# Attention pass on one Trainium2 core: three bf16 passes for the output projection, the value bias moved into the projection's bias row, and value transfers issued ahead of key transfers

## The chip, the core and the metric

The kernel runs on one core of one Trainium2 chip. The metric is the device time of one execution in microseconds (us). The core has a tensor engine (PE; its weight loads are shown apart, as PEld), a vector engine (DVE), a scalar engine (ACT), a general engine (POOL) and a synchronising engine (SP), which here only issues DMA transfers. Each engine works through its own instructions strictly in the order in which they were written. Engines meet only through semaphores: an instruction waits until a counter has reached a value, and everything that is queued behind it on its engine waits too.

## What is computed

Two layers over x of 128 sequences, 64 tokens and 256 channels. The change touches only the attention of the first layer:

```
x1 = LN(x) * (scale1 + 1) + shift1                  # scale1, shift1, gamma1 come from cond
q, k, v = x1 @ Wqkv + (q_bias, 0, v_bias)           # 16 heads of 16 channels
q = l2norm(q) * exp(min(scale_mul, log 100));  k = l2norm(k)
probs = softmax(q @ k^T)                            # per sequence and head, 64 x 64
o = probs @ v
x = x + (o @ Wproj + proj_b) * gamma1
```

Rows of probs sum to one, so a bias on v adds the same vector v_bias to every row of o, and (o + v_bias) @ Wproj + proj_b equals o @ Wproj + (proj_b + v_bias @ Wproj). A feed-forward part and a second layer of linear attention follow; the change leaves them as they are.

## The kernel before

The program is a setup and three passes in a row, each with a block of its own: attention, feed-forward, linear attention. A block begins only when all engines have finished the one ahead.

**A tile** is two sequences, 128 rows on the 128 partitions; there are 64 tiles. Most products are formed from operands split into a bf16 high part and a bf16 remainder: an engine writes the high part (HI), another subtracts it from the full value and writes the remainder (LO), and PE adds three products, HI*HI + HI*LO + LO*HI (`SPLITS`). The output projection is the exception: its operands are fp32.

**The order of work** in the attention pass is written out by hand. `pipeline(engine, stages)` takes a list of (lag, stage). In step S of the loop the engine runs each stage in the order of the list, on tile S - lag. Steps 0 to 75 are run; a middle part is a hardware loop of four steps a round. So within a step the list is the engine's queue order, and a wait holds all stages behind it. The lists before are:

- PE: scores (lag 8), project (11), turn_qk (5), probs_v (9), turn_o (10), qkv (3), turn_x (1)
- DVE: biases (4), modulate (2), v_low (4), outputs (10), reduce_norms (4), residual (11), hat (1), qk_lo (5), statistics (-1), aggregate (0)
- ACT: v_hi (4), square (4), modulate_second (2), high_exponentials (8), qk_hi (5), x1_high (2), full_exponentials (8), logs (4), o_copy (10), factor (4)
- POOL: normalise (5), rstd_of (1), add (12), x1_low (2), e_lo (8)
- SP: load_gain (9), place_k (5), place_v (5), each for two tiles in every second step

**Where the stages meet.** `qkv` (L779, L784, L787) writes a tile's products; the value half needs a matmul with the bias row (L784) ahead of its six. `v_hi` (ACT, L661) and `v_low` (DVE, L835) split it. `place_v` (L571) moves the split value of two tiles to `v_pairs` in 4 transfers, `place_k` (L553) the key to `k_pairs` in 8. A tile's slot of the split value is overwritten four tiles later, so `v_hi` waits until the transfers of that pair have landed. In the steady loop `place_v` itself waits only for `pv_done`, and `place_k` for `qk_lo_made`. `scores` (L760) waits for the key transfers; `high_exponentials` (L695) and `full_exponentials` (L700) write the exponential in bf16 and in fp32; `e_lo` (POOL, L627) subtracts one from the other, 1024 elements a partition. `probs_v` (L745), `outputs` (DVE, L840 and L845), `turn_o` (L734, a transpose into the second half of the bank `ps_x`) and `o_copy` (ACT, L706, to fp32) follow. `project` (PE, L722 and L724) needs `o_copy`, and the value split of the same step: its result shares a bank with the value, so it waits for `v_lo_made` of tile S - 4. `turn_qk` (L770), `qk_hi` (L681), `qk_lo` (L873) turn and split query and key. `residual` (DVE, L829) multiplies the projected tile by gamma1, `hat` (DVE, L881) normalises the next tile of x, SBUF to SBUF in fp32. The value half of `qkv` waits for `residual` of the same step, since they share the bank.

Of the kernel before, what the change touches and what calls it, by code (L numbers as in the profile page):

```python
# [22 lines left out]
ALU = mybir.AluOpType  # L23
# [83 lines left out]
class Shared:  # L107


    def __init__(self, nc, ctx):  # L110
        def sb(name, shape, dt):
# [14 lines left out]
        self.w_proj = sb("w_proj", [P, NC_, C], F32)  # L126
# [19 lines left out]
        self.bias_rows = sb("bias_rows", [P, 5 * C], BF16)  # L146
        self.rows_v, self.rows_proj, self.rows_qv3, self.rows_out3 = (
            self.bias_rows[:, a * C:b * C] for a, b in ((0, 1), (1, 2), (2, 4), (4, 5)))
# [13 lines left out]
def setup(nc, m, x, cond, qkv_w, q_bias, v_bias, scale_mul, proj_w, proj_b, ada_w, ada_b,  # L162
# [3 lines left out]
    with ExitStack() as ctx:  # L166
# [23 lines left out]
        bias_full = sb("bias_full", [P, 5 * C])  # L190
        bias_rest = sb("bias_rest", [P, 5 * C])
        bias_high = sb("bias_high", [P, 5 * C], BF16)
        bias_mid = sb("bias_mid", [P, 5 * C], BF16)
        band = sb("band", [P, P])
        ps = [ctx.enter_context(nc.psum_tensor(f"set_ps{i}", [P, 512], F32)) for i in range(6)]
# [9 lines left out]
        qkv_here = sem("qkv_here")  # L205
        qkv_hi_made = sem("qkv_hi_made")
# [25 lines left out]
        def _(sp):  # L232
            load(sp, [(cond_sb[:], cond)], cond_here)
            load(sp, [(w_ada[:], ada_w.rearrange(CHUNKED, p=P))], ada_here)
# [3 lines left out]
            load(sp, [(m.w_proj[:], proj_w.rearrange(CHUNKED, p=P))], attention_here)  # L238
# [5 lines left out]
            sp.wait_ge(attention_here, 16 * 2)  # L244

        @block.scalar
        def _(act):
            load(act, [(head_scale[:], scale_mul.rearrange("a h b c -> (a b c) h").to_broadcast([P, H]))], heads_here)
            load(act, [(bias_full[:, i * C:(i + 1) * C], row(b)) for i, b in enumerate((v_bias, proj_b, bq, bv, out_b))],
# [16 lines left out]
            act.activation(m.w_qkv[:, HI], qkv_full[:], ACT.Copy).then_inc(qkv_hi_made, 1)  # L266

        @block.gpsimd
        def _(pool):
# [24 lines left out]
            pool.tensor_tensor(m.w_qkv[:, LO], qkv_full[:], m.w_qkv[:, HI], ALU.subtract)  # L294
            pool.wait_ge(biases_split, 1)
# [7 lines left out]
        def _(pe):  # L303
# [5 lines left out]
            last.then_inc(transposed, 1)  # L309
            pe.wait_ge(cond_t_made, 1)  # L310
# [20 lines left out]
        def _(dve):  # L331
            dve.wait_ge(heads_here, 16)
# [13 lines left out]
            dve.wait_ge(biases_here, 16 * 5)  # L346
# [56 lines left out]
def attention_pass(nc, m, x, fc1_w):  # L403
# [10 lines left out]
    with ExitStack() as ctx:  # L414
# [30 lines left out]
        o_t = sb("o_t", [P, 2, SEQ, L])  # L445
# [13 lines left out]
        ps_xt, ps_ot = ps_x[:, 0:C], ps_x[:, C:2 * C]  # L459
        ps_vv, ps_y = ps_v[:, 0:C], ps_v[:, C:2 * C]  # L460
# [39 lines left out]
        o_t_made = sem("o_t_made")  # L500
# [18 lines left out]
        def _(sp):  # L519
# [56 lines left out]
            pipeline(sp, [(9, load_gain), (5, place_k), (5, place_v), (0, load_later)])  # L576
# [57 lines left out]
        def _(act):  # L634
# [67 lines left out]
            def o_copy(t):  # L702
                a = t.slot(2)
                act.wait_ge(o_turned, t.n + 1)
                reuse(act, proj_done, t, 2)
                act.activation(o_t[a][:], ps_ot.rearrange("p (s g q) -> p g s q", s=SEQ, g=2), ACT.Copy  # L706
                               ).then_inc(o_t_made, 1)
# [4 lines left out]
                           (2, x1_high), (8, full_exponentials), (4, logs), (10, o_copy), (5, split_fc1),  # L712
# [3 lines left out]
        def _(pe):  # L716
            def project(t):
                a = t.slot(2)
                pe.wait_ge(o_t_made, t.n + 1)
# [53 lines left out]
            def qkv(t):  # L773
# [976 lines left out]
```

## Time and profile before

| What | Value |
|---|---|
| Median of 3 runs | 1348.47 us (1347.26 to 1349.31) |
| Profiled execution: its own time, its span | 1349.81 us, 1347.9 us |
| Granted TensorE clock, mean share of full speed | 0.967 |
| PE busy | 1152.5 us, 86% |
| PEld busy | 856.6 us, 64% |
| DVE busy | 994.8 us, 74% |
| ACT busy | 867.3 us, 64% |
| POOL busy | 933.9 us, 69% |
| Setup | 0 to about 38.8 us |
| Attention pass | about 38.8 to 527 us |
| The two other passes | about 527 to 1347.9 us |

The busy shares are means over passes with different limits; the change lies in the first two stretches only. A timeline row gives the start in us, the time in us, engine, line, operation, what is written and read, the shapes and the count; a bracket behind it tells how long the engine stood idle ahead of it and which operation let it go. Consecutive operations of one engine overlap a little, so the distance from one start to the next is often shorter than the duration.

### The profile page before, as it was taken

How to read it: one execution, taken by the hardware profiler on the slowest of the kernel's cores; microseconds unless marked ns; L12 is line 12 of the kernel's file. 1: busy time of each engine (PE TensorE's matmuls, PEld its weight loads, DVE VectorE, ACT ScalarE, POOL GpSimd, SP SyncE). 2: the span in 40 equal slices, each digit the busy share in tenths (PEclk: the TensorE clock that was granted, in tenths of full speed). 3: DMA queues.
4: the chain of work that ended last, by engine and by line, in shares of the span. 5: the costliest groups of instructions: out<-in, count | busy, mean ns of one | idle time of the engine just before them, and what ended most of it. 6: DMA issues, size and time to landing. Idle time of an engine off the chain costs nothing. (4 is left out here: it accounts for less than half of the span.)

```text
span 1347.9 us, 38178 instructions
## 1 busy us (share of the span) xinstructions
PE 1152.5 (86%) x12189; PEld 856.6 (64%) x12342; DVE 994.8 (74%) x2388; ACT 867.3 (64%) x2268; POOL 933.9 (69%) x1091
## 2 busy tenths in 40 slices
PE   2568898998989874899999999978888888888886
PEld 1356777777777763466666666655666666666664
DVE  2857787887878754745556465439999999999993
ACT  1456677777777762545454544528888888888884
POOL 3547677777777755656575765635788888888888
PEclk9789999999999997899999999989999999999997
DMA  5454233232333332110101001000011111111112
GB/s 149 152 112 117 56 52 62 54 60 56 57 61 53 65 54 66 40 32 16 32 16 31 18 29 32 17 16 7 24 37 51 35 35 50 36 37 36 52 36 71
DMA packets 142704, 67.73 MB, mean 50 GB/s; under 512 B 80688, under 2 KB 141360, under 8 KB 142640
## 3 DMA queue, kind: packets, MB, share of 16 engines
q1 hardware_dynamic: 109472, 40.53, 14.2%
q10 hardware_dynamic: 33168, 26.38, 6.9%
q8 instruction: 35, 0.57, 0.2%
q14 instruction: 29, 0.24, 0.1%
HBM read 41.18 MB, written 8.65 MB: 37 GB/s over the span
## 5 line engine op out<-in xcount | busy, mean ns | idle before, releaser
L1107 PE MATMUL f_ps_y<-w_fc,f_h_split 128*128 128x256 bf16 x1536 | 172.7, 273 | 1.4 <-DVE f_branch L1213 1.4
L1134 PE MATMUL f_ps_h<-f_x_split,w_fc 128*128 128x512 bf16 x737 | 165.8, 381 | 3.1 <-DVE f_x_split L1187 1.5
L1107 PEld LDWEIGHTS f_ps_y<-w_fc,f_h_split 128*128 128x128 bf16 x1536 | 150.2, 98 | 22.5 <-issue 1.7
L627 POOL TENSOR_TENSOR e_split<-e_full,e_split 128x1024 bf16<-128x1024 f32 x64 | 136.6, 2135 | 32.7 <-ACT e_full L700 31.6
L1221 DVE TENSOR_TENSOR f_h_split<-f_h,f_h_split 128x512 bf16<-128x512 f32 x64 | 65.0, 1018 | 103.0 <-ACT f_h L1091 103.0
L1090 ACT ACTIVATE f_h_split<-f_ps_h,b_fc 128x512 bf16<-128x512 f32 x128 | 89.0, 695 | 66.0 <-POOL f_h_split L1045 32.6
L1134 PEld LDWEIGHTS f_ps_h<-f_x_split,w_fc 128*128 128x128 bf16 x768 | 75.4, 98 | 87.0 <-issue 2.2
L609 POOL TENSOR_TENSOR x_split<-x_t,x_split 128x256 bf16<-128x256 f32 x64 | 44.6, 697 | 104.4 <-ACT x_split L649 104.4
L760 PE MATMUL ps_s<-qk_t,k_pairs 128*128 128x64 bf16 x3072 | 101.7, 194 | 11.7 <-DMA k_pairs<-qk_t 9.8
L760 PEld LDWEIGHTS ps_s<-qk_t,k_pairs 128*128 128x128 bf16 x3072 | 99.0, 99 | 14.5 <-DMA k_pairs<-qk_t 11.0
L1045 POOL TENSOR_TENSOR f_h_split<-f_h,f_h_split 128x512 bf16<-128x512 f32 x64 | 80.6, 1269 | 36.3 <-ACT f_h L1091 36.3
L1560 PE MATMUL l_ps_qv<-w_qvk,l_x_split 128*128 128x512 bf16 x383 | 94.4, 383 | 4.9 <-DVE l_v_split L1672 1.5
L661 ACT ACTIVATE v_split<-ps_v 128x256 bf16<-128x256 f32 x64 | 24.8, 387 | 108.1 <-DMA v_pairs<-v_split 86.6
L1091 ACT ACTIVATE f_h<-f_ps_h,b_fc 128x512 f32<-128x512 f32 x128 | 89.5, 699 | 0.0
L779 PE MATMUL ps_qk<-w_qkv,x_split 128*128 128x512 bf16 x323 | 83.3, 390 | 5.3 <-POOL x_split L609 1.1
L1078 ACT ACTIVATE f_x_split<-f_x 128x1024 bf16<-128x1024 f32 x16 | 16.9, 1057 | 107.9 <-POOL f_x L1000 107.9
L1430 ACT ACTIVATE l_z_t<-l_ps_yt,shift,scale 128x64 f32<-128x64 f32 x256 | 83.5, 425 | 4.3 <-PE l_ps_yt L1509 3.2
L1464 ACT ACTIVATE l_kq<-l_ps_k,l_k_shift 128x64 f32<-128x64 f32 x256 | 76.9, 313 | 11.5 <-DVE l_k_shift L1652 11.5
L695 ACT ACTIVATE e_split<-ps_s,minus_shift 128x1024 bf16<-128x1024 f32 x64 | 71.5, 1117 | 10.2 <-PE ps_s L760 9.9
L1521 PE MATMUL l_ps_y<-l_kv_split,l_kq_t 128*64 128x128 bf16 x768 | 41.6, 222 | 39.8 <-DVE l_y_hat L1609 39.8
L1368 POOL TENSOR_TENSOR l_kv_split<-l_kv,l_kv_split 128x512 bf16<-128x512 f32 x64 | 73.9, 1155 | 0.2 <-ACT l_kv_split L1443 0.2
L1450 ACT ACTIVATE l_kq_t<-l_ps_kq 128x512 bf16<-128x512 f32 x64 | 38.2, 597 | 53.1 <-PE l_ps_kq L1549 53.1
(171 smaller groups left out, 3416.1 us busy)
## 6 DMA issues: line engine op xcount, KB each, us to landing
v_pairs<-v_split SPq DMA_DIRECT2D x128, 66.0 KB, 2.1
k_pairs<-qk_t SPq DMA_DIRECT2D x256, 32.0 KB, 2.2
gain<-gammas SPq DMA_DIRECT2D x64, 128.0 KB, 3.0
f_gain<-gammas ACTq DMA_DIRECT2D x32, 256.0 KB, 4.3
l_gate<-in_cond ACTq DMA_DIRECT2D x128, 64.0 KB, 2.6
out<-x_all ACTq DMA_DIRECT2D x16, 512.0 KB, 2.9
x_all<-in_x SPq DMA_DIRECT2D x13, 512.0 KB, 6.5
w_ada<-in_L_cond_ada_w SPq DMA_DIRECT2D x1, 1536.0 KB, 8.3
```

Source lines behind the costliest of these rows:

```text
L627: pool.tensor_tensor(flat(e_split[a][:, LO]), flat(e_full[:]), flat(e_split[a][:, HI]), ALU.subtract).then_inc(e_lo_made, 1)
L760: last = pe.matmul(ps_s[:, s, G_ * c + g], k_pairs[:, t.slot(4), k, c, s, g].rearrange("p r k -> p (r k)"), qk_t[:, 0, t.slot(4), q, c, s ...
L779: last = pe.matmul(ps_qk[:, :], x1_split[a][:, xs, c, :], m.w_qkv[:, ws, c, 0:2 * C], start=(i == 0 and c == 0), stop=(i == 2 and c == NC_ ...
L1045: pool.tensor_tensor(h_split[a][:, LO, f], h[f % 4][:], h_split[a][:, HI, f], ALU.subtract).then_inc(h_lo_odd, 1)
L1090: act.activation(h_split[a][:, HI, f], ps_h[f % 4][:], ACT.Gelu, bias=m.b_fc1[:, f:f + 1])
L1091: act.activation(h[f % 4][:], ps_h[f % 4][:], ACT.Gelu, bias=m.b_fc1[:, f:f + 1]).then_inc(h_made, 1)
L1107: last = pe.matmul(ps_y[:, i], h_split[a][:, hs, f, i * P:(i + 1) * P], m.w_fc2[:, ws, f], start=(f == 0 and k == 0), stop=(f == F_CHUNKS ...
L1134: last = pe.matmul(ps_h[f % 4][:], m.w_fc1[:, ws, c, f * P:(f + 1) * P], x2_split[a][:, xs, c], start=(k == 0 and c == 0), stop=(k == 2 an ...
L1368: pool.tensor_tensor(kv_split[a][:, LO], kv[a][:], kv_split[a][:, HI], ALU.subtract).then_inc(kv_lo_made, 1)
L1430: act.activation(z_t[a][:, c, s * L:(s + 1) * L], ps_yt[:, c, s * L:(s + 1) * L], ACT.Identity, bias=by_seq(m.shift3, c, t, s), scale=by_s ...
L1464: act.activation(kq[t.slot(4)][:, i * L:(i + 1) * L], ps_k[:, c, s * L:(s + 1) * L], ACT.Exp, bias=k_shift[a][:, c, s:s + 1], accum_out=su ...
L1560: last = pe.matmul(ps_qv[:], x3_split[a][:, xs, c], m.w_qvk3[:, ws, c, 0:2 * C], start=False, stop=(i == 2 and c == NC_ - 1))
```

## The change

1. **Projection.** The projection weight is split in the setup into bf16 high part and remainder. `o_copy` becomes `o_hi` (ACT, same place in its list, writes bf16), and a new stage `o_low` on DVE subtracts it from the transposed output in PSUM. `project` runs six bf16 matmuls of 256 columns in place of two fp32 ones (four entries in the trace). What waited for `o_t_made` (`project`, `turn_o`, `turn_x`) waits for `o_lo_made`.
2. **Value bias.** The setup forms v_bias @ Wproj with two fp32 matmuls on a widened bias and adds it to proj_b; the row of v_bias goes from the loop, and with it one matmul of 256 columns a tile. The bias buffers hold 4 rows of 256 instead of 5.
3. **Transfers.** `place_v` stands ahead of `place_k` in SP's list.

The diff, without declarations:

```diff
@@ -231,22 +239,23 @@
             load(sp, [(cond_sb[:], cond)], cond_here)
+            load(sp, [(proj_full[:], proj_w.rearrange(CHUNKED, p=P))], proj_here)
             load(sp, [(w_ada[:], ada_w.rearrange(CHUNKED, p=P))], ada_here)
...
             load(sp, [(w_emb[:], emb_w.rearrange(CHUNKED, p=P))], emb_here)
-            load(sp, [(m.w_proj[:], proj_w.rearrange(CHUNKED, p=P))], attention_here)
             sp.wait_ge(gammas_made, 1)
...
             load(sp, [(m.x_all[:, part], x_tiles(x)[:, part])], m.x_here[1])
-            sp.wait_ge(attention_here, 16 * 2)
+            sp.wait_ge(attention_here, 16)

...
             load(act, [(head_scale[:], scale_mul.rearrange("a h b c -> (a b c) h").to_broadcast([P, H]))], heads_here)
-            load(act, [(bias_full[:, i * C:(i + 1) * C], row(b)) for i, b in enumerate((v_bias, proj_b, bq, bv, out_b))],
+            load(act, [(b_v[:], column(v_bias))], proj_here)
+            load(act, [(bias_full[:, i * C:(i + 1) * C], row(b)) for i, b in enumerate((proj_b, bq, bv, out_b))],
                  biases_here)
@@ -264,6 +273,8 @@
             act.activation(m.w_qkv[:, HI], qkv_full[:], ACT.Copy).then_inc(qkv_hi_made, 1)
+            act.wait_ge(proj_here, 16 * 2)
+            act.activation(m.w_proj[:, HI], proj_full[:], ACT.Copy).then_inc(proj_hi_made, 1)

@@ -292,6 +303,8 @@
             pool.tensor_tensor(m.w_qkv[:, LO], qkv_full[:], m.w_qkv[:, HI], ALU.subtract)
+            pool.wait_ge(proj_hi_made, 1)
+            pool.tensor_tensor(m.w_proj[:, LO], proj_full[:], m.w_proj[:, HI], ALU.subtract)
             pool.wait_ge(biases_split, 1)
@@ -307,6 +320,11 @@
             last.then_inc(transposed, 1)
+            pe.wait_ge(v_bias_widened, 1)
+            pe.wait_ge(proj_here, 16 * 2)
+            for c in range(NC_):
+                last = pe.matmul(ps[5][:, 0:C], b_v_wide[:, c], proj_full[:, c], start=(c == 0), stop=(c == NC_ - 1))
+            last.then_inc(v_bias_carried, 1)
             pe.wait_ge(cond_t_made, 1)
@@ -329,6 +347,8 @@
         def _(dve):
+            dve.wait_ge(proj_here, 16 * 2)
+            dve.tensor_copy(b_v_wide[:], b_v[:, :, None].to_broadcast([P, NC_, P])).then_inc(v_bias_widened, 1)
             dve.wait_ge(heads_here, 16)
@@ -343,7 +363,10 @@

-            dve.wait_ge(biases_here, 16 * 5)
+            dve.wait_ge(biases_here, 16 * 4)
+            dve.wait_ge(v_bias_carried, 1)
+            dve.tensor_tensor(bias_full[:, 0:C], bias_full[:, 0:C], ps[5][:, 0:C], ALU.add).then_inc(proj_bias_summed, 1)
+            dve.wait_ge(proj_bias_summed, 1)
             dve.tensor_copy(bias_high[:], bias_full[:]).then_inc(biases_split, 1)
@@ -457,6 +480,7 @@
         ps_xt, ps_ot = ps_x[:, 0:C], ps_x[:, C:2 * C]
+        turned_o = ps_ot.rearrange("p (s g q) -> p g s q", s=SEQ, g=2)
         ps_vv, ps_y = ps_v[:, 0:C], ps_v[:, C:2 * C]
@@ -573,7 +598,7 @@

-            pipeline(sp, [(9, load_gain), (5, place_k), (5, place_v), (0, load_later)])
+            pipeline(sp, [(9, load_gain), (5, place_v), (5, place_k), (0, load_later)])
             sp.wait_ge(x_updated, TILES)
@@ -699,36 +724,36 @@

-            def o_copy(t):
+            def o_hi(t):
                 a = t.slot(2)
...
                 reuse(act, proj_done, t, 2)
-                act.activation(o_t[a][:], ps_ot.rearrange("p (s g q) -> p g s q", s=SEQ, g=2), ACT.Copy
-                               ).then_inc(o_t_made, 1)
+                act.activation(o_t[a][:, HI], turned_o, ACT.Copy).then_inc(o_hi_made, 1)

...
             pipeline(act, [(4, v_hi), (4, square), (2, modulate_second), (8, high_exponentials), (5, qk_hi),
-                           (2, x1_high), (8, full_exponentials), (4, logs), (10, o_copy), (5, split_fc1),
+                           (2, x1_high), (8, full_exponentials), (4, logs), (10, o_hi), (5, split_fc1),
                            (4, factor)])
...
                 a = t.slot(2)
-                pe.wait_ge(o_t_made, t.n + 1)
+                pe.wait_ge(o_lo_made, t.n + 1)
                 reuse(pe, branch_made, t, 1)
...
                 pe.matmul(ps_y, m.ones[:], m.rows_proj, start=True, stop=False)
-                for g in range(2):
-                    last = pe.matmul(ps_y, o_t[a][:, g].rearrange("p s q -> p (s q)"), m.w_proj[:, g, :],
-                                     start=False, stop=(g == 1))
+                for i, (os, ws) in enumerate(SPLITS):
+                    for g in range(2):
+                        last = pe.matmul(ps_y, o_t[a][:, os, g].rearrange("p s q -> p (s q)"), m.w_proj[:, ws, g],
+                                         start=False, stop=(i == 2 and g == 1))
                 last.then_inc(proj_done, 1)
...
                 pe.wait_ge(o_made, t.n + 1)
-                reuse(pe, o_t_made, t, 1)
+                reuse(pe, o_lo_made, t, 1)
                 bank_free(pe, x1_second, t, 8, SEQ)
@@ -781,18 +806,17 @@
                 bank_free(pe, branch_made, t, -8)
-                pe.matmul(ps_vv, m.ones[:], m.rows_v, start=True, stop=False)
                 for i, (xs, ws) in enumerate(SPLITS):
...
                         last = pe.matmul(ps_vv, x1_split[a][:, xs, c, :], m.w_qkv[:, ws, c, 2 * C:3 * C],
-                                         start=False, stop=(i == 2 and c == NC_ - 1))
+                                         start=(i == 0 and c == 0), stop=(i == 2 and c == NC_ - 1))
                 last.then_inc(qkv_done, 1)
...
                 reuse(pe, x1_second, t, 1, SEQ)
-                bank_free(pe, o_t_made, t, -9)
+                bank_free(pe, o_lo_made, t, -9)
                 for c in range(NC_):
@@ -847,6 +871,12 @@

+            def o_low(t):
+                a = t.slot(2)
+                dve.wait_ge(o_hi_made, t.n + 1)
+                reuse(dve, proj_done, t, 2)
+                dve.tensor_tensor(o_t[a][:, LO], turned_o, o_t[a][:, HI], ALU.subtract).then_inc(o_lo_made, 1)
+
             def statistics(t):
@@ -893,7 +923,7 @@
             pipeline(dve, [(4, biases), (2, modulate), (4, v_low), (10, outputs), (4, reduce_norms),
-                           (11, residual), (1, hat), (5, qk_lo), (-1, statistics), (0, aggregate), (1, clear_k)])
+                           (10, o_low), (11, residual), (1, hat), (5, qk_lo), (-1, statistics), (0, aggregate), (1, clear_k)])

```

DVE, a step of the attention pass in the fill of the pipeline, from the norms of query and key to the next value split (L808/L832 and L810/L834 norms, L829/L853 `residual`, L881/L911 `hat`, L873/L903 `qk_lo`), before:

```order
L808 TENSOR_REDUCE norms<-squares 128x32 [waits logs_made,squared]
L810 SCALAR_TENSOR_TENSOR norms<-norms,norm_weight 128x32 [waits norms_made]
L829 TENSOR_TENSOR branch<-ps_v,gain 128x256 [waits gain_here0,proj_done]
L881 TENSOR_SCALAR x_hat<-x_all,mean_var,rstd 128x256 [waits x_hat_t,rstd_made]
L873 TENSOR_TENSOR qk_t<-ps_qkt,qk_t 128x2x256 [waits qk_hi_made]
```

and after:

```order
L832 TENSOR_REDUCE norms<-squares 128x32 [waits logs_made,squared]
L834 SCALAR_TENSOR_TENSOR norms<-norms,norm_weight 128x32 [waits norms_made]
L878 TENSOR_TENSOR o_t<-ps_x,o_t 128x256 [waits o_hi_made]
L853 TENSOR_TENSOR branch<-ps_v,gain 128x256 [waits gain_here0,proj_done]
L911 TENSOR_SCALAR x_hat<-x_all,mean_var,rstd 128x256 [waits x_hat_t,rstd_made]
L903 TENSOR_TENSOR qk_t<-ps_qkt,qk_t 128x2x256 [waits qk_hi_made]
```

The new row L878 (`o_low`) with its wait for ACT stands ahead of `residual`, `hat` and `qk_lo`.

SP, one round of the steady loop (two of its four steps), before:

```order
L529 DMA gain<-gammas 64x2x256
L548 ISA
L553 DMA k_pairs<-qk_t 16x16x64 [waits qk_lo_made]
L553 DMA k_pairs<-qk_t 16x16x64 x7
L571 DMA v_pairs<-v_split 64x2x264 [waits pv_done]
L571 DMA v_pairs<-v_split 64x2x264 x3
```

and after:

```order
L554 DMA gain<-gammas 64x2x256
L413 ISA
L596 DMA v_pairs<-v_split 64x2x264 [waits pv_done]
L596 DMA v_pairs<-v_split 64x2x264 x3
L573 REGISTER_ALU
L578 DMA k_pairs<-qk_t 16x16x64 [waits qk_lo_made]
L578 DMA k_pairs<-qk_t 16x16x64 x7
```

The four value transfers and their wait stand ahead of the eight key transfers.

## Rows read from the trace of the kernel before

**Rows 1.** List of waits, 100 to 450 us: total us, times, longest us.

```profile
ACT v_split L661 <- DMA v_pairs<-v_split: 66.6, 25, 4.8
```

**Rows 2.** Timeline, end of a step; columns: start us, us, engine, line, operation.

```profile
299.59 1.11 ACT L700 ACTIVATE e_full<-ps_s,minus_shift 128x1024 f32<-128x1024 f32 x1
299.72 2.61 SPq L571 DMA_DIRECT2D v_pairs<-v_split  x4
299.77 0.67 POOL L609 TENSOR_TENSOR x_split<-x_t,x_split 128x256 bf16<-128x256 f32 x1 [0.36 <-ACT x_split L649]
...
299.83 0.76 DVE L881 TENSOR_SCALAR x_hat<-x_all,mean_var,rstd 128x256 f32 x1
300.51 0.68 DVE L873 TENSOR_TENSOR qk_t<-ps_qkt,qk_t 128x512 bf16<-128x512 f32 x1
...
300.70 0.38 ACT L706 ACTIVATE o_t<-ps_x 128x256 f32<-128x256 f32 x1
300.77 2.14 POOL L627 TENSOR_TENSOR e_split<-e_full,e_split 128x1024 bf16<-128x1024 f32 x1 [0.33 <-ACT e_full L700]
...
300.99 0.82 PE L787 MATMUL ps_v<-w_qkv,x_split 128*128 128x256 bf16 x6
301.11 0.41 DVE L860 BATCH_NORM_STATS2 stats<-x_all 128x6 f32 x1
...
301.52 0.65 DVE L888 TENSOR_TENSOR qk<-ps_qk,b_qk 128x512 f32<-128x512 f32 x1
...
301.64 0.38 PE L797 MATMUL ps_x<-ident,x_hat 128*128 128x128 f32 x2
```

**Rows 3.** Timeline, the step after it and part of the next.

```profile
303.82 0.39 ACT L661 ACTIVATE v_split<-ps_v 128x256 bf16<-128x256 f32 x1 [2.52 <-DMA v_pairs<-v_split]
...
304.36 0.43 DVE L835 TENSOR_TENSOR v_split<-ps_v,v_split 128x256 bf16<-128x256 f32 x1 [1.46 <-ACT v_split L661]
...
304.84 0.28 PE L722 MATMUL ps_v<-bias_rows,ones 128*128 128x256 bf16 x1 [1.42 <-DVE v_split L835]
...
304.96 1.03 PE L724 MATMUL ps_v<-w_proj,o_t 128*128 128x256 f32 x4
...
305.83 0.60 PE L770 MATMUL ps_qkt<-ident,qk_hat 128*128 128x128 f32 x4
...
306.46 0.60 ACT L681 ACTIVATE qk_t<-ps_qkt 128x512 bf16<-128x512 f32 x1
...
306.90 0.42 DVE L829 TENSOR_TENSOR branch<-ps_v,gain 128x256 f32<-128x256 f32 x1
...
307.24 0.40 DVE L881 TENSOR_SCALAR x_hat<-x_all,mean_var,rstd 128x256 f32 x1
307.26 1.11 ACT L700 ACTIVATE e_full<-ps_s,minus_shift 128x1024 f32<-128x1024 f32 x1
...
308.27 5.28 SPq L553 DMA_DIRECT2D k_pairs<-qk_t  x8
...
309.54 1.56 PE L760 MATMUL ps_s<-qk_t,k_pairs 128*128 128x64 bf16 x48
...
309.88 0.60 DVE L820 TENSOR_SCALAR x_t<-ps_x,scale,shift 128x64 f32<-128x64 f32 x2 [0.43 <-PE ps_x L797]
310.39 0.42 DVE L835 TENSOR_TENSOR v_split<-ps_v,v_split 128x256 bf16<-128x256 f32 x1
...
312.35 0.91 PE L745 MATMUL ps_o<-v_pairs,e_split 128*128 128x66 bf16 x24
```

**Rows 4.** Instructions of line 829 (the branch), whole program; durations ns min/median/max.

```profile
L829 DVE TENSOR_TENSOR branch<-ps_v,gain x64: 423/424/426, 99.7 to 525.7; 128x256 f32<-128x256 f32 x64
```

**Rows 5.** Timeline, the branch of the last step that still splits a value.

```profile
492.97 0.42 DVE L829 TENSOR_TENSOR branch<-ps_v,gain 128x256 f32<-128x256 f32 x1
```

**Rows 6.** Busy times of one window: us busy (count) per engine, PE clock, DMA.

```profile
110.00:120.00 10.00, 7.30 (x135) 6.05 (x132) 6.28 (x16) 4.79 (x11) 8.20 (x11) 1.00 0.50 84
```

**Rows 7.** Timeline of the setup: the widest step of the bias split.

```profile
25.97 4.32 DVE L349 TENSOR_TENSOR bias_rest<-bias_full,bias_high 128x1280 f32<-128x1280 f32 x1
```

More of the change, by code:

```diff
@@ L125, in __init__ @@
         self.w_qkv = sb("w_qkv", [P, 2, NC_, 3 * C], BF16)
-        self.w_proj = sb("w_proj", [P, NC_, C], F32)
+        self.w_proj = sb("w_proj", [P, 2, NC_, C], BF16)
         self.w_fc1 = sb("w_fc1", [P, 2, NC_, D_FF], BF16)
@@ L145, in __init__ @@
         self.ones = sb("ones", [P, P], BF16)
-        self.bias_rows = sb("bias_rows", [P, 5 * C], BF16)
-        self.rows_v, self.rows_proj, self.rows_qv3, self.rows_out3 = (
-            self.bias_rows[:, a * C:b * C] for a, b in ((0, 1), (1, 2), (2, 4), (4, 5)))
+        self.bias_rows = sb("bias_rows", [P, 4 * C], BF16)
+        self.rows_proj, self.rows_qv3, self.rows_out3 = (
+            self.bias_rows[:, a * C:b * C] for a, b in ((0, 1), (1, 3), (3, 4)))
         self.b_fc1 = sb("b_fc1", [P, D_FF // P], F32)
@@ L189, in setup @@
         qkv_full = sb("qkv_full", [P, NC_, 3 * C])
[L190 to L193, printed above, removed]
+        bias_full = sb("bias_full", [P, 4 * C])
+        bias_rest = sb("bias_rest", [P, 4 * C])
+        bias_high = sb("bias_high", [P, 4 * C], BF16)
+        bias_mid = sb("bias_mid", [P, 4 * C], BF16)
         band = sb("band", [P, P])
+        proj_full = sb("proj_full", [P, NC_, C])
+        b_v = sb("b_v", [P, NC_])
+        b_v_wide = sb("b_v_wide", [P, NC_, P])
         ps = [ctx.enter_context(nc.psum_tensor(f"set_ps{i}", [P, 512], F32)) for i in range(6)]
@@ L205, in setup @@
         qkv_here = sem("qkv_here")
+        proj_here = sem("proj_here")
+        proj_hi_made = sem("proj_hi_made")
+        v_bias_widened = sem("v_bias_widened")
+        v_bias_carried = sem("v_bias_carried")
+        proj_bias_summed = sem("proj_bias_summed")
         qkv_hi_made = sem("qkv_hi_made")
@@ L444, in attention_pass @@
         o_full = sb("o_full", [P, SEQ, C // 2], F32, 1)[0]
-        o_t = sb("o_t", [P, 2, SEQ, L])
+        o_t = sb("o_t", [P, 2, 2, SEQ, L], BF16)
         gain = sb("gain", [P, 4, C], F32, 1)[0]
@@ L499, in attention_pass @@
         o_turned = sem("o_turned")
-        o_t_made = sem("o_t_made")
+        o_hi_made = sem("o_hi_made")
+        o_lo_made = sem("o_lo_made")
         proj_done = sem("proj_done")
@@ L1729, in laid_out @@
         return a.reshape(1, 2, H // 2, 1).swapaxes(1, 2).reshape(1, H, 1, 1)
+    if name == "L0_cond_v_bias":
+        return a.reshape(2, H // 4, 2, HD).transpose(2, 1, 0, 3).reshape(C)
     if name == "L0_cond_proj_w":
```

## The prediction

> **What bounds the kernel now.** I read the busy table first: PE leads with 86%, but as a mean over three passes. The change touches the setup and the attention pass, so I read the list of waits of the steady part of that pass. Its largest wait that holds up everybody is one for a transfer: ACT's `v_hi` waits 66.6 us, in 25 waits, for value transfers to land, once in two steps [rows 1]. The timeline shows how [rows 2, 3]. In the step that begins with the scores near 302 us, the four value issues end at 299.72 + 2.61 = 302.33, ACT gets on at 303.82, that is 1.49 later, and DVE's `v_low` (304.36) and PE's projection (304.84) follow in a row. The next step has no such wait: from one `v_low` to the next, 304.36 to 310.39, it is 6.03 us. The mean step is longer: the branch of step 11 starts at 99.7 and that of step 67 at 492.97 [rows 4, 5], 393.3 us for 56 steps, 7.02 a step. The sum has to say what the 56 become.
>
> **The projection on PE.** From the bias matmul to the transposes behind it are 305.83 - 304.84 = 0.99 us [rows 3]. The new form keeps the bias matmul (0.12 to the next start) and has six bf16 matmuls of 256 columns, the form of the value half, 301.64 - 300.99 = 0.65 [rows 2]. That is 0.77, so 0.22 less. The value half loses its bias matmul, another 0.12. PE gets 0.34 a step, worth something only where PE ends last.
>
> **The new stage on DVE.** `o_low` has exactly the form of `v_low` (PSUM and bf16 in, bf16 out, 256 elements), 0.43 us [rows 3]; 0.34 to the next start, as from the branch to `hat`, 306.90 to 307.24. The cost is not in the 0.34 but in its place. It waits for `o_hi` of the same step, and ACT reaches that copy only behind `full_exponentials`: 299.59 to 300.70, 1.11 after that one's start [rows 2]. In the step of rows 3 DVE has done its branch at 306.90 and its `hat` at 307.24, before ACT has even begun `full_exponentials` (307.26). Queued behind the new wait are `residual`, `hat`, `qk_lo`, `statistics`, and then `biases`, `modulate` and `v_low` of the next step. The projection of the next step waits for that `v_low`, `turn_qk` is behind the projection, `qk_hi` behind `turn_qk`, and `full_exponentials` and `o_hi` behind `qk_hi`. So the wait closes a ring through all of DVE's second half, PE and ACT, once a step, without slack.
>
> **A hold within the ring.** `hat` now comes while POOL runs `e_lo`, which it never does in the rows of before. When they meet, it costs. At 299.83 `hat` was recorded with 0.76 us instead of 0.40, while POOL's fp32-to-bf16 subtraction ran from 299.77 to 300.44 [rows 2, 3]: its own 0.40 began at 300.19, 0.25 ahead of POOL's recorded end. `e_lo` is the same kind of subtraction, four times as long. The statistics at 301.11 ran at 0.41 in the middle of an `e_lo`, so not every DVE operation is held; those that read PSUM are not either (301.52, 0.65) [rows 2].
>
> The Trainium skill, SBUF — State Buffer, section "SBUF: two separate sides", says that VectorE and GpSimd share a pair of ports by an exclusive lock, held for the whole instruction of the one that came first. The trace agrees that `hat` is held, but has it start 0.25 before the recorded end; by the page's rule to the letter each step would be 0.25 longer and the sum 1427.
>
> **The ring, added up** from the start of `full_exponentials` to the next. `e_lo` starts 300.77 - 299.59 = 1.18 later and takes 2.14; `hat` gets on 0.25 before its end: 3.07. Then `qk_lo` 0.32 (300.51 - 300.19), `statistics` 0.60 (301.11), `biases` 0.41 (301.52), all [rows 2]; `modulate` 0.60, as for the other 512-element operation, 300.51 to 301.11; `v_low` 0.51 (309.88 to 310.39), projection 0.48 (304.36 to 304.84), transposes 0.77 (above), `qk_hi` 0.63 (305.83 to 306.46), `full_exponentials` 0.80 (306.46 to 307.26) [rows 3]. Sum: 3.07 + 0.32 + 0.60 + 0.41 + 0.60 + 0.51 + 0.48 + 0.77 + 0.63 + 0.80 = 8.19 us a step. Without the hold the first term is 1.11 to `o_hi`, 0.54 to `o_low` (ACT to DVE as 303.82 to 304.36), 0.34 to the branch and 0.34 to `hat`: 2.33 in place of 3.07, so 7.45.
>
> I checked what else could be later than the ring. `residual` starts 1.99 after `full_exponentials` and ends at 2.42; the value half of `qkv` (0.65) and the transposes of x (0.38) follow and end near 3.5, while `modulate` wants them at 3.07 + 0.32 + 0.60 + 0.41 + 0.60 = 5.0: hidden. Scores start near 3.3 and end 1.56 later, at 4.9; the projection comes at 6.0: hidden, so PE's 0.34 buys nothing. POOL works behind `e_lo` on what is needed at 6.8.
>
> **The transfers.** Value transfers first removes the wait of [rows 1]: they are issued after `pv_done`, long before they are needed. The key transfers then start when `qk_lo` is done, 3.07 + 0.32 + 0.68 = 4.07, take 5.28 to issue and 1.49 to land: 10.84. The scores that need them come two steps on, at 8.19 + 3.3 = 11.5. A slack of 0.7; where issues are slower, as they are near the start of the pass, the key may be late by some tenths, which I leave to the range. So the wait removed (about 0.9 a step over the 6.03) is replaced by a longer one.
>
> **Sum.** Of the 56 steps the last two have no `hat`: 2.33 - 0.34 + 0.60 (`biases`) + 0.60 + 0.51 + 0.48 + 0.77 + 0.63 + 0.80 = 6.4 to 6.7; I take 6.7. 54 x 8.19 + 2 x 6.7 = 455.7, against 393.3: 62 more. Behind step 67 a few projections wait for `o_low` directly, about 0.6 each, less the shorter matmuls: 2 more. Setup: the bias split shrinks by a fifth (its widest part 4.32 us [rows 7]) and gains an add of 0.4; PE's two extra fp32 matmuls and the wait for the weight lie where PE waits anyway; one more column load of single elements stands in ACT's queue. I put it at 0, between -1.5 and +2. Against the execution profiled, 1349.8 + 64 = 1414; that execution is 1.3 above the median of the runs, so the median should be **1413**.
>
> Uncertain terms: the handoffs between engines in the ring vary by about 0.05 each, four of them, so 0.2 a step, 11 us either way; key transfers late by 0.3 in each second step add 8.
>
> **Rivals.**
>
> *Not held.* If `hat` gets through beside `e_lo`, the step is 7.45 and the sum 54 x 7.45 + 13.4 - 393.3 + 2 = +24: 1373. For it: only short holds stand in the trace. Against: they fit the end of POOL's work. Chance 0.10.
>
> *Not slower.* The mechanism: ACT's `o_hi` is ready when DVE gets to `o_low`, so no ring forms, and only the exchange of transfers counts. Then the queue of SP bounds: scores to the end of `probs_v` is 312.35 + 0.91 - 309.54 = 3.72, less 0.22, then 2.61 for the value issues, 5.28 for the key issues, 1.49 to land and about 0.1 between: 13.0 for two steps [rows 2, 3]. 28 pairs are 364, 29 less than now: 1319. It decides if `o_hi` came before 306.90 in rows 3, and ACT's list forbids that, since its `full_exponentials` stands ahead and starts at 307.26. Chance 0.06; with something between, near no change, 0.02.
>
> *The clock.* PE is busy at most 6.03 - 0.34 = 5.7 of 8.19 us, 70%, in pieces with two pauses of about 1 us. In the window from 110 to 120 it was busy 7.30 of 10 us and the granted clock stayed at 1.00 [rows 6], the level of 2.4 GHz. If it fell to 1.2 GHz for good, the six matmuls and the transposes of the ring would double, 0.77 + about 0.5: +71, 1484. If it does so in a quarter of the steps, 1431. Chance of more than that 0.07.
>
> **How the numbers follow.** The ring with the hold has 0.75. Range: 1392 to 1440, from the ring's 11 either way, the late key and a partial hold below; it leaves out the unheld case, the fast one and a clock lost for long. A measurement can tell about 0.2% (3 us) from no change: faster 0.06, within 0.02, slower 0.92.
>
> **What would show it.** Right: DVE idle ahead of L878, released by ACT's L731, about 1 to 2 us a step; L911 (`hat`) recorded at about 1.4 us instead of 0.40; branches 8.2 us apart, even and odd steps alike; ACT's wait for value transfers gone; the six matmuls 0.65 from start to start of the transposes. Wrong: no idle time ahead of L878; `hat` at 0.4; steps that still come in pairs of unequal length, with PE waiting for key transfers; a granted clock well under 1.00.

## The result, and the profile after

| | Before | Changed |
|---|---|---|
| Median | 1347.95 us (1347.26 to 1349.31, 4 runs) | 1415.76 us (1414.55 to 1418.05, 4 runs) |
| Ratio | 1 | 1.0504 (95% interval 1.0486 to 1.0522) |
| Span of the profiled execution | 1347.9 us | 1416.0 us |
| Granted TensorE clock, mean | 0.967 | 0.966 |

The changed kernel is 5.0% slower. Where the 68 us of span come from can be read by following one operation through both traces, the branch on DVE (line 829 before, 853 after), with the branch rows of the two other passes. These are answers on single lines of the changed kernel (durations in ns min/median/max, first and last start) and rows of its timeline:

```profile
L853 DVE TENSOR_TENSOR branch<-ps_v,gain x64: 411/414/425, 95.3 to 592.0; 128x256 f32<-128x256 f32 x64
```

```profile
555.68 0.41 DVE L853 TENSOR_TENSOR branch<-ps_v,gain 128x256 f32<-128x256 f32 x1
```

```profile
L1243 DVE TENSOR_TENSOR f_branch<-f_ps_y,b_fc x15: 1223/1225/1225, 648.3 to 950.5; 128x1024 f32<-128x1024 f32 x15
L1620 DVE TENSOR_TENSOR l_branch<-l_ps_out,l_gate x64: 409/411/425, 1021.4 to 1411.4; 128x256 f32<-128x256 f32 x64
```

The branch of step 11 starts at 95.30 instead of 99.7 [rows 4]: setup and fill are 4.4 us shorter. That of step 67 starts at 555.68 instead of 492.97 [rows 5]: the 56 steps between them take 460.4 us instead of 393.3, 8.22 a step instead of 7.02, and that is 67.1 us more. The last branch of the pass comes at 592.0 instead of 525.7 [rows 4]: 3.6 more in the drain. From there to the end 1.8 more come in, in passes that were not changed, in small pieces: before, the first branch of the feed-forward started at 581.3, and those of the last pass ran from 954.2 to 1343.4, so 0.6, 0.3 and 0.8 of it lie in these three stretches. -4.4 + 67.1 + 3.6 + 1.8 = 68.1. So the loss lies in the steps of the attention pass. Two of the 56 steps, those that begin at 161.20 and 195.48, took 9.6 us each at a lower TensorE clock (see below); the last two took 13.3 together, and the other 52 took 8.23 each.

What the steps wait for is in the list of waits from 100 to 450 us of the changed kernel (total us, times, longest us):

```profile
POOL x_split L634 <- ACT x_split L674: 103.1, 42, 3.7
DVE o_t L878 <- ACT o_t L731: 82.2, 42, 3.2
ACT v_split L686 <- PE ps_v L811: 67.5, 42, 1.7
ACT squares L680 <- DVE qk L918: 58.6, 42, 1.5
PE ps_v L811 <- DVE branch L853: 43.1, 42, 1.1
```

ACT's wait for value transfers, 66.6 us and first among the transfers' waits before [rows 1], is gone. In its place DVE waits in every step, 1.96 us each, for ACT's `o_hi`, and the other rows show who waits behind it: PE for the branch, ACT for `qk`. The timeline of one step shows the whole ring (start us, us, engine, line, operation):

```profile
302.03 1.13 ACT L725 ACTIVATE e_full<-ps_s,minus_shift 128x1024 f32<-128x1024 f32 x1
...
303.15 0.41 ACT L731 ACTIVATE o_t<-ps_x 128x256 bf16<-128x256 f32 x1
303.32 2.12 POOL L652 TENSOR_TENSOR e_split<-e_full,e_split 128x1024 bf16<-128x1024 f32 x1 [0.34 <-ACT e_full L725]
...
303.68 0.42 DVE L878 TENSOR_TENSOR o_t<-ps_x,o_t 128x256 bf16<-128x256 f32 x1 [1.84 <-ACT o_t L731]
304.02 0.41 DVE L853 TENSOR_TENSOR branch<-ps_v,gain 128x256 f32<-128x256 f32 x1
304.35 1.25 DVE L911 TENSOR_SCALAR x_hat<-x_all,mean_var,rstd 128x256 f32 x1
...
305.52 0.68 DVE L903 TENSOR_TENSOR qk_t<-ps_qkt,qk_t 128x512 bf16<-128x512 f32 x1
...
306.12 0.41 DVE L890 BATCH_NORM_STATS2 stats<-x_all 128x6 f32 x1
...
306.53 0.65 DVE L918 TENSOR_TENSOR qk<-ps_qk,b_qk 128x512 f32<-128x512 f32 x1
...
307.11 0.58 DVE L844 TENSOR_SCALAR x_t<-ps_x,scale,shift 128x64 f32<-128x64 f32 x2
...
307.61 0.41 DVE L859 TENSOR_TENSOR v_split<-ps_v,v_split 128x256 bf16<-128x256 f32 x1
...
308.08 0.28 PE L746 MATMUL ps_v<-bias_rows,ones 128*128 128x256 bf16 x1 [0.42 <-DVE v_split L859]
...
308.85 0.60 PE L795 MATMUL ps_qkt<-ident,qk_hat 128*128 128x128 f32 x4
...
309.58 0.60 ACT L706 ACTIVATE qk_t<-ps_qkt 128x512 bf16<-128x512 f32 x1
...
310.38 1.11 ACT L725 ACTIVATE e_full<-ps_s,minus_shift 128x1024 f32<-128x1024 f32 x1
```

From 302.03 to 310.38 are 8.35 us, and each row begins when the one before it in the ring lets it. One of these handoffs is nearly a tie. ACT has a way of its own from `biases` to `qk_hi`, over the squares, `modulate_second` and `high_exponentials`, which ends with

```profile
308.45 1.11 ACT L720 ACTIVATE e_split<-ps_s,minus_shift 128x1024 bf16<-128x1024 f32 x1
```

at 309.56, against 309.45 for PE's transposes and 309.58 for the start of `qk_hi`. By these rows the part of the ring from `biases` to `qk_hi` could hardly be shortened on DVE and PE alone; no run tried it. `hat` (L911) is recorded with 1.25 us instead of 0.40. It begins inside POOL's L652, which runs from 303.32 to 305.44, and ends at 305.60, 0.16 behind it.

### The profile page after: what moved, and what is told of

Its sections match the earlier page's. It is cut to its first block and busy times, and to the rows that moved or that the text cites. A ratio compares the mean times of both kernels' runs of the same rounds, so it can differ in the third digit from the quotient of the medians.

```text
span 1416.0 us, 38589 instructions
## 1 busy us (share of the span) xinstructions
PE 1174.1 (83%) x12410; PEld 840.8 (59%) x12410; DVE 1034.8 (73%) x2454; ACT 874.8 (62%) x2269; POOL 937.0 (66%) x1092
## 5 line engine op out<-in xcount | busy, mean ns | idle before, releaser
L1164 PE MATMUL f_ps_h<-f_x_split,w_fc 128*128 128x512 bf16 x768 | 173.5, 383 | 0.9 <-DVE f_x_split L1217 0.9
L652 POOL TENSOR_TENSOR e_split<-e_full,e_split 128x1024 bf16<-128x1024 f32 x64 | 136.0, 2124 | 38.8 <-ACT e_full L725 38.8
L878 DVE TENSOR_TENSOR o_t<-ps_x,o_t 128x256 bf16<-128x256 f32 x64 | 27.2, 424 | 135.4 <-ACT o_t L731 135.4
L785 PE MATMUL ps_s<-qk_t,k_pairs 128*128 128x64 bf16 x3072 | 105.8, 197 | 15.4 <-DMA k_pairs<-qk_t 12.4
L785 PEld LDWEIGHTS ps_s<-qk_t,k_pairs 128*128 128x128 bf16 x3072 | 102.1, 100 | 20.5 <-DMA k_pairs<-qk_t 13.6
L811 PE MATMUL ps_v<-w_qkv,x_split 128*128 128x256 bf16 x384 | 52.8, 273 | 56.8 <-DVE branch L853 56.8
L804 PE MATMUL ps_qk<-w_qkv,x_split 128*128 128x512 bf16 x384 | 95.8, 387 | 2.1 <-DVE qk L918 1.6
L680 ACT ACTIVATE squares<-qk 128x512 f32<-128x512 f32 x64 | 40.3, 630 | 82.2 <-DVE qk L918 82.2
L811 PEld LDWEIGHTS ps_v<-w_qkv,x_split 128*128 128x128 bf16 x384 | 33.5, 98 | 89.1 <-issue 48.0
```

The source lines that it names most:

```text
L652: pool.tensor_tensor(flat(e_split[a][:, LO]), flat(e_full[:]), flat(e_split[a][:, HI]), ALU.subtract).then_inc(e_lo_made, 1)
L785: last = pe.matmul(ps_s[:, s, G_ * c + g], k_pairs[:, t.slot(4), k, c, s, g].rearrange("p r k -> p (r k)"), qk_t[:, 0, t.slot(4), q, c, s ...
L804: last = pe.matmul(ps_qk[:, :], x1_split[a][:, xs, c, :], m.w_qkv[:, ws, c, 0:2 * C], start=(i == 0 and c == 0), stop=(i == 2 and c == NC_ ...
L1164: last = pe.matmul(ps_h[f % 4][:], m.w_fc1[:, ws, c, f * P:(f + 1) * P], x2_split[a][:, xs, c], start=(k == 0 and c == 0), stop=(k == 2 an ...
```

## The experiments

Two questions were open: whether the place of `o_low` is the cause, and whether `hat` is really held by POOL or is only long in the record. Beside them stood what the exchange of the transfers is worth. Each kernel was timed in rounds with the kernel before; ratios are to that kernel, with their 95% interval.

### e1: o_low last on DVE

```diff
-                           (10, o_low), (11, residual), (1, hat), (5, qk_lo), (-1, statistics), (0, aggregate), (1, clear_k)])
+                           (11, residual), (1, hat), (5, qk_lo), (-1, statistics), (0, aggregate), (10, o_low), (1, clear_k)])
```

> The changed kernel with one edit: DVE's o_low stands last in its list (behind the statistics) instead of ahead of the branch. My theory (a ring through DVE, PE and ACT that o_low's place closes): no ring is left, DVE meets o_hi when it is made, hat runs ahead of e_lo again at 0.40 us. What bounds then is the queue of SP, about 13.0 us for two steps, so 6.5 to 6.6 a step: 56 x (8.22 - 6.55) = 94 less than the changed kernel's 1416, near 1322, faster than before. Rival (the extra stage costs by being there at all, or the split weights do): the time stays above 1395.

Measured: 1332.49 us (1330.99 to 1335.16), ratio 0.9872 (0.9846 to 0.9898). The same work in another order is 83 us faster than the changed kernel and 1.3% faster than the kernel before. It is 10 us above my 1322. In the steady part two steps take 13.25 us and not 13.1, since the queue of SP takes a little more than I had counted; that is 28 x 0.15 = 4. The rest lies near the start of the pass, where single steps take up to 8.9 us. Its timeline, scores, transfers and scores again (the view ends at 314, so the last row shows 10 of its 48 matmuls):

```profile
300.46 1.57 PE L785 MATMUL ps_s<-qk_t,k_pairs 128*128 128x64 bf16 x48 [0.70 <-DMA k_pairs<-qk_t]
...
303.07 0.91 PE L770 MATMUL ps_o<-v_pairs,e_split 128*128 128x66 bf16 x24
...
304.01 2.60 SPq L596 DMA_DIRECT2D v_pairs<-v_split  x4
...
306.73 5.26 SPq L578 DMA_DIRECT2D k_pairs<-qk_t  x8
...
313.72 0.46 PE L785 MATMUL ps_s<-qk_t,k_pairs 128*128 128x64 bf16 x10 [0.77 <-DMA k_pairs<-qk_t]
```

From scores to scores are 13.26 us for two steps: 3.52 to the end of `probs_v` at 303.98, then 2.60 and 5.26 of issues with 0.15 of gaps, and 1.73 from the end of the last issue to the scores. So this kernel is bound by the transfers' queue, and PE waits for keys.

### e2: the exchange of the transfers alone, in the kernel before

```diff
-            pipeline(sp, [(9, load_gain), (5, place_k), (5, place_v), (0, load_later)])
+            pipeline(sp, [(9, load_gain), (5, place_v), (5, place_k), (0, load_later)])
```

> The kernel before with only the transfers exchanged: value transfers ahead of key transfers. My theory: the wait of v_hi for value transfers is gone, the scores wait for key transfers instead; two steps are 3.72 + 0.1 + 2.61 + 5.28 + 1.49 = 13.2 us instead of 13.8 in the steady part, 14.04 in the mean: 28 x 0.84 = 24 less, 1324. Rival (the new wait costs as much as the old): 1345 to 1351. A second rival (only DVE and PE bound then, no wait left): 56 x (7.02 - 6.03) = 55 less, 1293.

Measured: 1338.25 us (1336.15 to 1340.45), ratio 0.9908 (0.9884 to 0.9933). The direction is as expected, the size is less than half: 11 us instead of 24. Issues of its SP queue and its main wait (list from 110 to 450 us):

```profile
310.61 5.24 SPq L553 DMA_DIRECT2D k_pairs<-qk_t  x8
...
324.13 5.26 SPq L553 DMA_DIRECT2D k_pairs<-qk_t  x8
```

```profile
PE ps_s L760 <- DMA k_pairs<-qk_t: 30.5, 25, 2.0
```

Two steps take 13.52 us here and 13.47 on average in the steady part, not 13.2; before they took 13.8. The wait for values (66.6 us in 25 waits from 100 us) has become one of PE for keys (30.5 us in 25 waits from 110 us). The exchange shifts the bound from one transfer to the other, and the gain is the small difference. My 24 was made against the mean of 14.04, which holds longer steps near the start. They stay: the 56 steps take 384.1 us, a mean of 13.72 for two, so the exchange gains 9.2 in them. It gains another 8.5 ahead of step 11, whose branch starts at 91.23 instead of 99.72, and loses 8.5 again in the drain, 41.2 instead of 32.7, where the scores wait for keys.

Between this kernel and e1 stand the other two parts of the change, the projection and the value bias. Their steady pairs differ by 0.22 us, 13.47 and 13.25, and their times by 6 us. The intervals of the two ratios overlap a little, so the traces suggest a small worth of the saved PE work, and the times do not show it for certain.

### e3: hat ahead of o_low

```diff
-                           (10, o_low), (11, residual), (1, hat), (5, qk_lo), (-1, statistics), (0, aggregate), (1, clear_k)])
+                           (1, hat), (10, o_low), (11, residual), (5, qk_lo), (-1, statistics), (0, aggregate), (1, clear_k)])
```

> The changed kernel with one edit: hat stands ahead of o_low on DVE. My theory (ring, with hat held 0.85 us by POOL's e_lo): hat leaves the ring, and with it the hold; the step falls by 0.34 + 0.85 = 1.19 us, 54 x 1.19 = 64 less, 1352. Rival (the ring without a hold; hat is long in the record for another reason): only 0.34 a step, 1398. Rival (no ring, DVE is bound by its own work): no change, 1416, as the sum of DVE's work is the same.

Measured: 1350.71 us (1347.77 to 1354.33), ratio 1.0006 (0.9992 to 1.0020). The ring is still there (DVE's L878 waits for ACT in 48 of the 48 steps between 110 and 450 us), but it is 65 us shorter in all, and `hat` is back at 0.41 us:

```profile
DVE o_t L878 <- ACT o_t L731: 72.5, 48, 1.9
```

```profile
L911 DVE TENSOR_SCALAR x_hat<-x_all,mean_var,rstd 128x256 f32 x44 | 18.0, 410 | 1.6
```

(The second row is from the groups of DVE from 90 to 550 us: busy us, mean ns, idle before.) Had DVE been bound by the sum of its work, nothing would have changed. The gain is more than three times the 0.34 a step that `hat` takes in the sequence (54 x 0.34 = 18), so the hold was on the path too.

### e4: key transfers first, in the changed kernel

```diff
-            pipeline(sp, [(9, load_gain), (5, place_v), (5, place_k), (0, load_later)])
+            pipeline(sp, [(9, load_gain), (5, place_k), (5, place_v), (0, load_later)])
```

> The changed kernel with the transfers in the order of before, key ahead of value. My theory: at 8.2 us a step the value transfers land about 9.4 + 2.6 + 1.5 = 13.5 us after the start of a full_exponentials, and v_low asks for them at 13.3 (the step after next but one): 0 to 0.5 late in every second step, 1416 to 1430. If the ring left no room beside the transfers as in the kernel before (2.5 us in every second step): near 1480.

Measured: 1438.41 us (1437.16 to 1439.10), ratio 1.0652 (1.0629 to 1.0676), so 23 us more than the changed kernel and 8 above the top of what I expected. The wait for values is back even at this pace:

```profile
ACT v_split L686 <- DMA v_pairs<-v_split: 78.2, 20, 5.4
```

```profile
320.61 5.27 SPq L578 DMA_DIRECT2D k_pairs<-qk_t  x8
...
325.92 2.61 SPq L596 DMA_DIRECT2D v_pairs<-v_split  x4
...
330.12 0.39 ACT L686 ACTIVATE v_split<-ps_v 128x256 bf16<-128x256 f32 x1 [3.65 <-DMA v_pairs<-v_split]
```

The keys of this round began at 320.61, those of the round before at 303.74: 16.87 for two steps, where the changed kernel takes 16.49 in the same part. The 0.38 is within what I expected, 28 x 0.38 = 11; the range was missed elsewhere. The branch of step 11 starts at 100.27, 5.0 later than in the changed kernel, and the ten steps from there take 91.4 us instead of 83.7, single ones up to 11.45. A longer step gives the transfers no room, since they begin only when `qk_lo` is done, 4.2 us after the start of `full_exponentials` (1.0 before [rows 3]). So within the changed kernel the exchange is worth 23 us, and it is not what made it slow.

### e5: hat behind qk_lo

```diff
-                           (10, o_low), (11, residual), (1, hat), (5, qk_lo), (-1, statistics), (0, aggregate), (1, clear_k)])
+                           (10, o_low), (11, residual), (5, qk_lo), (1, hat), (-1, statistics), (0, aggregate), (1, clear_k)])
```

> The changed kernel with one edit: hat stands behind qk_lo on DVE instead of ahead of it. The ring keeps all its members and DVE all its work; only the moment changes at which hat meets e_lo: about 0.6 us later, when e_lo has 0.2 us left. Theory of the hold: hat falls from 1.25 to about 0.55 us in the record, the step from 8.22 to about 7.55, 54 x 0.67 = 36 less than 1416, 1380. Rival (hat is long because DVE's statistics buffer or the clock makes it so, or its cost is hidden): 1414 to 1418.

Measured: 1384.20 us (1382.56 to 1385.90), ratio 1.0252 (1.0235 to 1.0269): 32 us less than the changed kernel with all members of the ring kept. The answers on `hat`'s line, changed kernel ahead, this kernel behind:

```profile
L911 DVE TENSOR_SCALAR x_hat<-x_all,mean_var,rstd x64: 397/1251/1581, 38.8 to 534.8; 128x256 f32 x44, 128x256 f32<-128x256 f32 x20
```

```profile
L911 DVE TENSOR_SCALAR x_hat<-x_all,mean_var,rstd x64: 398/654/1145, 38.8 to 505.9; 128x256 f32 x44, 128x256 f32<-128x256 f32 x20
```

The median falls from 1251 to 654 ns, 0.60 us, and 54 x 0.60 = 32. The mean step falls from 8.22 to 7.69. Only the moment changed at which `hat` meets `e_lo`. This is the cleanest evidence for the hold.

### e6: o_hi earlier on ACT, DVE as in the changed kernel

```diff
-                           (2, x1_high), (8, full_exponentials), (4, logs), (10, o_hi), (5, split_fc1),
+                           (2, x1_high), (10, o_hi), (8, full_exponentials), (4, logs), (5, split_fc1),
```

> The changed kernel with one edit on ACT alone: o_hi stands ahead of full_exponentials; DVE's list stays. Theory (DVE waits for o_hi's place on ACT): from turn_qk to turn_qk the ring is 1.85 to o_hi, then 0.54, 0.34, 0.34, 0.32, 0.60, 0.41, 0.60, 0.51, 0.48, 0.77: 6.76, and hat meets no e_lo, since that starts later. 56 x (8.22 - 6.76) = 82 less, 1334; where the queue of SP with its 13.26 us for two steps ends later, no lower than 1332. Rival (the ring is closed by something else, as the value half's wait for the branch): less than 20 us gained, above 1396.

Measured: 1330.98 us (1329.51 to 1331.61), ratio 0.9861 (0.9844 to 0.9877), 85 us less than the changed kernel with DVE's list untouched. Its timeline:

```profile
308.03 0.38 ACT L731 ACTIVATE o_t<-ps_x 128x256 bf16<-128x256 f32 x1
308.31 1.11 ACT L725 ACTIVATE e_full<-ps_s,minus_shift 128x1024 f32<-128x1024 f32 x1
308.44 0.43 DVE L878 TENSOR_TENSOR o_t<-ps_x,o_t 128x256 bf16<-128x256 f32 x1 [0.76 <-ACT o_t L731]
308.78 0.41 DVE L853 TENSOR_TENSOR branch<-ps_v,gain 128x256 f32<-128x256 f32 x1
309.12 0.40 DVE L911 TENSOR_SCALAR x_hat<-x_all,mean_var,rstd 128x256 f32 x1
...
309.49 2.14 POOL L652 TENSOR_TENSOR e_split<-e_full,e_split 128x1024 bf16<-128x1024 f32 x1 [0.81 <-ACT e_full L725]
```

`hat` now starts ahead of POOL's subtraction and takes 0.40 us. What the queues do to each other is decided by the pair of places, that of `o_hi` on ACT and that of `o_low` on DVE; moving either is enough.

### e7: one more matmul in the value half

```diff
+                pe.matmul(ps_vv, m.ones[:], m.zeros[:], start=True, stop=False)
                 for i, (xs, ws) in enumerate(SPLITS):
```

> The changed kernel with a bias matmul put back at the head of the value half, on a buffer of zeros (0.12 us of PE a step). Theory (PE's work in the value half is hidden behind DVE's part of the ring, with 1.5 us to spare): no change, 1414 to 1418. Rival (the value half ends last, through the value split): 64 x 0.12 = 8 more, 1424.

The start mark moves from the first of the six matmuls to the new one, and the setup clears one more buffer. Measured: 1415.14 us (1414.13 to 1415.77), ratio 1.0486 (1.0468 to 1.0503), the changed kernel's own 1415.76 within the spread. The bias matmul that the change takes out of every tile buys nothing in it.

### e8: three value transfers ahead of the keys, the fourth behind them, on top of e1

`place_v` issues three of its four transfers, and a new stage the fourth:

```diff
-                    for r in range(2):
+                    for r in range(2 - s):
...
-            pipeline(sp, [(9, load_gain), (5, place_v), (5, place_k), (0, load_later)])
+            pipeline(sp, [(9, load_gain), (5, place_v), (5, place_k), (5, place_v_last), (0, load_later)])
```

> The kernel of e1 (o_low last), with three of the four value transfers ahead of the key transfers and the fourth behind them. Theory (the queue of SP bounds e1: 3.52 to the end of probs_v, 2.6 and 5.26 to issue, 1.73 to land, 13.26 for two steps): the keys start one issue of 0.65 earlier, and the last value lands about 0.5 us after the scores' start, when v_low does not need it yet. 12.6 for two steps, 28 x 0.65 = 18 less than 1332.5, 1314. Rival (PE and DVE bound e1 already): 1330 to 1333. Rival (the last value comes too late): 1335 to 1345.

Measured: 1312.63 us (1311.97 to 1313.44), ratio 0.9724 (0.9708 to 0.9740), the fastest kernel of the study, 2.8% below the kernel before. Its SP queue:

```profile
306.71 5.23 SPq L578 DMA_DIRECT2D k_pairs<-qk_t  x8
311.98 0.64 SPq L606 DMA_DIRECT2D v_pairs<-v_split  x1
...
319.40 5.23 SPq L578 DMA_DIRECT2D k_pairs<-qk_t  x8
```

Two steps take 12.69 us, 0.57 less than in e1, close to the 0.65 of one issue. So the queue did bound e1, and PE and DVE had room for one issue less. ACT now waits for the fourth value transfer in every second step (43.8 us in 26 waits from 110 to 450 us), but that costs nothing: `v_low` starts 0.85 us after the scores in such a step as in the other.

## Why the prediction held

The forecast was 1413 us in a range of 1392 to 1440; measured were 1415.8.

*The ring.* Forecast as 8.19 us a step, measured 8.23 in the 52 undisturbed steps that hold it. Its members are seen in the timeline above, and e1 and e6 break it from either side, on DVE and on ACT, and give back 83 and 85 us. That the place of the wait costs and not the 0.43 us of work is shown by e1, which has the same work.

*The hold.* Forecast: `hat` gets on 0.25 us before POOL's recorded end, so its record is about 1.4 us. Measured 1.25; it ends at 305.60, its own 0.40 began at 305.20, 0.24 before POOL's end at 305.44. e3 and e5 show that the time is real: moved out of `e_lo` or nearer to its end, `hat` gives back what the theory said, 65 us (64 expected) and 32 us (36 expected). By the rule that the Trainium skill states in SBUF — State Buffer, section "SBUF: two separate sides" (the pair is held for the whole instruction), taken to the letter, the sum would have been 1427. The trace agrees that there is a hold, and is 0.24 a step short of its whole length. Which DVE operations are held was inferred from durations alone; no run here changed the kind of `hat`.

*What is hidden.* The forecast said that PE's saving of 0.34 us a step buys nothing. That is shown for the 0.12 of the value half: PE waits for the branch 1.0 us in each step, and e7 adds a matmul without effect. It does not hold for the other 0.22, which lie in the projection. The projection is a member of the ring, and the forecast's own sum counts it at the new 0.77 and not at 0.99; no run puts the old projection back into this kernel. The check of the hidden work also left out a wait, that of PE's transposes of x for `hat` of the same step:

```profile
305.82 0.43 PE L821 MATMUL ps_x<-ident,x_hat 128*128 128x128 f32 x2 [0.51 <-DVE x_hat L911]
306.09 1.56 PE L785 MATMUL ps_s<-qk_t,k_pairs 128*128 128x64 bf16 x48
```

The scores therefore start 4.06 after `full_exponentials` and not 3.3, and end at 5.6 and not 4.9. The projection comes at 6.05, so this is still hidden, but the room is 0.4 and not 1.1.

*The transfers.* Forecast: the wait for values goes, and the keys land 0.7 us before they are asked for. Between 100 and 450 us the changed kernel has no wait for keys. With the 1.73 of e1 from the last issue they land at 306.22 + 5.26 + 1.73 = 313.2, and the scores that need them start at 314.34, so the slack is 1.1; it is larger than forecast because the scores come later. e4 puts the exchange at 23 us within the changed kernel. The fast rival, which had the queue of SP as its bound and 1319 us, sits near e6 (1331), whose only difference is the copy's place: its mechanism was right, its price 12 us too low. Of these, 7 come from the steady pairs, 13.25 in e6 and not 13.0: in e1's trace issues to landing and scores take 1.73 us instead of the 1.49 that I read from the value transfers, and gaps add 0.15. The rest lies in longer steps near the start of the pass.

*Where terms were off.* Setup and fill were put at 0, between -1.5 and +2. They came out at -4.4. Setup itself is 1.9 shorter: the first statistics of the attention pass start at 36.93,

```profile
36.93 0.89 DVE L890 BATCH_NORM_STATS2 stats<-x_all 128x6 f32<-128x256 f32 x2 [0.30 <-PEq L166]
```

instead of 38.81 before. ACT's queue gets through its column loads earlier, not later as I feared. Much of that is not the change's: e2, which has the setup of before, starts these statistics at 37.67. The other 2.5 are in the fill, and there it is the exchange that saves: e4, without it, has 4.5 more than the changed kernel from the first statistics to the branch of step 11. The steps, on the other side, came out at 460.4 us and not 455.7. The last two took 13.3, as forecast (13.4). Of the 4.7 the two steps at a lower clock make 2.7, and 52 steps that are 0.04 longer make 2. The drain is 3.6 longer and not 2: there the scores wait for keys that now stand behind the values, at worst

```profile
574.12 2.74 PE L785 MATMUL ps_s<-qk_t,k_pairs 128*128 128x64 bf16 x48 [6.16 <-DMA k_pairs<-qk_t]
```

and in e4, with keys first, the drain is 2.5 shorter. From the change's window on, the two unchanged passes add 1.8 us that I cannot name. The errors are -4.4, +4.7, +1.6 and +1.8. They cancel in part: that the sum came within 3 us of the median is luck, while the ring itself, off by 0.04 us a step, is not.

*The clock.* The forecast put PE's share at 70% and left a clock lost for long out of its range. By the records PE is busy 77% of the time from 220 to 450 us, and the granted clock is 1.00 there, the level of 2.4 GHz. It did fall to the level of 1.2 GHz in two short stretches of the steady part, near 164 and 198 us; the last section has the rows.

## What to carry to other kernels

Where each engine works through a list written by hand, an added operation costs its place, not its duration: look at which position of the other engine's list makes its input, compare the two clock times in the trace of before, and if the input comes later, add up the ring that closes. Here one subtraction of 0.43 us cost 83 us in one place, while in another the kernel with it was faster than the kernel before. A reordering also brings operations together that never overlapped before: check the pairs on DVE and POOL for records that are long only when they meet. And when one transfer's wait is removed by exchanging two, ask when the other one lands; splitting the first (e8) gave another 20 us on top of e1, more than the whole of e1 had gained over the kernel before.

## What the runs showed of the hardware that was not expected

- In every step of the steady part DVE's fp32 `hat` (SBUF to SBUF) was held by POOL's subtraction, 0.85 us in most steps and 0.77 in each fourth. `o_low` (0.42) and the branch (0.41), which read PSUM, ran beside the same subtraction unchanged, and so did the statistics before (0.41 at 301.11 [rows 2]). The own 0.40 us of `hat` began 0.24 to 0.27 us ahead of POOL's recorded end, at a hold of 0.85 us, at one of 0.36 (before) and at those of 0.16 to 0.26 in e5 alike. Whether the hold ends early or POOL's record ends late can't be told from these traces.
- In the profiled execution of the changed kernel the granted clock stood at 1.00 from 110 to 120, with PE busy 7.64 of 10 us, and fell for a few us in two later steps:

```profile
110.00:120.00 10.00, 7.64 (x106) 5.24 (x103) 6.60 (x17) 6.71 (x15) 6.67 (x8) 1.00 0.26 52
164.00:168.00 4.00, 4.00 (x59) 3.59 (x57) 3.09 (x9) 2.44 (x4) 1.31 (x3) 0.59 0.09 32
```

```profile
163.62 2.57 PE L785 MATMUL ps_s<-qk_t,k_pairs 128*128 128x64 bf16 x48 [0.17 <-issue]
```

  The scores took 2.57 us instead of 1.56, and the step 9.58 instead of about 8.25. The step near 198 us did the same (0.57 from 198 to 202). In the four us ahead of the first fall PE was busy 2.41. The kernel before fell too between 152 and 172 us, and e7, which differs by one matmul, did not between 95 and 450 us; what brings it on these runs do not show.

- From the end of the last key issue to the first matmul that needs it were 1.73 us, against 1.49 from the last value issue to ACT before, and 1.59 in e4.
